# A decoder of two layers on one core: output chains in later slots, the first mixture's norm and router logits inside attention slots

## The reference, cut

```python
x = _layernorm(x + _L0_attn_ref(x, ...))          # window of 16 around a token, 16 heads of 8; token 0 sees all
x = _layernorm(x + _L0_xattn_ref(x, ctx, ...))    # causal self attention + attention on ctx, one output product
x = _layernorm(x + _L0_ffn_ref(x, ...))           # 16 experts, each takes its top 64 tokens of 1024
x = _layernorm(x + _L1_attn_ref(x, ...))          # gated linear recurrence and a gated MLP
x = _layernorm(x + _L1_xattn_ref(x, ctx, ctx, ...))
x = _layernorm(x + _L1_ffn_ref(x, ...))           # 8 experts, top 2 of them per token

# the opening of _L0_ffn_ref, which the change is about
rms = jnp.sqrt(jnp.mean(xf * xf, axis=-1, keepdims=True) + EPS)
xn = xf / rms * norm_weight
logits = xn @ router_weight.T + router_bias
_, idx = jax.lax.top_k(logits.T, top_k)           # top_k = 64
```

## Time and profile before

| | us |
|---|---|
| median of 3 timed runs | 622.6 |
| lowest, highest | 620.65, 623.71 |
| the profiled execution | 616.85 |
| its span, first to last instruction | 615.1 |

### The profile page before, as it was taken

The page is one execution under the profiler, slowest core; times in us unless marked ns, Lnnn a source line. Parts: engine busy times, 40 slices in busy tenths (PEclk is TensorE's granted clock), DMA queues, the critical chain, the costliest instruction groups (busy, mean ns, idle before and its releaser), DMA issues. The chain is left out here.

```text
span 615.1 us, 10513 instructions
## 1 busy us (share of the span) xinstructions
PE 503.2 (82%) x3848; PEld 239.5 (39%) x3848; DVE 382.2 (62%) x876; ACT 221.5 (36%) x447; POOL 182.3 (30%) x296
## 2 busy tenths in 40 slices
PE   3899988878989898852499957885998889789994
PEld 2445443333333333320159843363333333334441
DVE  7646756577675768147965678644478842255574
ACT  2213452454656556701012115222117654332221
POOL 7736365644473622125000025101434000000000
PEclk9999998999999999977789978896899986799998
DMA  6321012235411100025040022000311000425200
GB/s 229 89 61 52 4 52 55 69 114 165 140 54 52 36 19 3 3 67 243 2 138 2 2 66 89 0 2 14 90 52 53 4 3 0 143 64 150 58 17 18
DMA packets 26899, 38.03 MB, mean 62 GB/s; under 512 B 3648, under 2 KB 19520, under 8 KB 26464
## 3 DMA queue, kind: packets, MB, share of 16 engines
q1 hardware_dynamic: 26848, 37.36, 20.0%
HBM read 23.91 MB, written 0.59 MB: 40 GB/s over the span
## 5 line engine op out<-in xcount | busy, mean ns | idle before, releaser
L1052 DVE TENSOR_REDUCE nmax<-bank 128x2 f32<-128x512 f32 (+2 forms) x240 | 145.6, 625 | 80.6 <-PE bank L832 38.3
L940 ACT ACTIVATE arena<-bank 128x512 f32<-128x512 f32 (+2 forms) x256 | 130.0, 524 | 136.0 <-PE bank L836 94.6
L498 PE MATMUL bank<-causal_qk,identb 128*128 128x512 bf16 x309 | 99.6, 428 | 28.9 <-DVE moe_top L1330 16.0
L836 PE MATMUL bank<-arena 64*128 64x256 bf16 (+2 forms) x512 | 87.0, 262 | 1.6 <-ACT arena L940 1.5
L832 PE MATMUL bank<-arena 62*128 62x256 bf16 (+2 forms) x512 | 85.2, 258 | 3.6 <-DVE nmax L1052 3.2
L877 PE MATMUL bank<-arena 128*32 128x256 f32 (+4 forms) x1088 | 75.3, 356 | 7.2 <-ACT arena L940 4.4
L832 PEld LDWEIGHTS bank<-arena 62*128 62x128 bf16 x512 | 30.1, 95 | 67.5 <-issue 49.3
L498 PEld LDWEIGHTS bank<-causal_qk,identb 128*128 128x128 bf16 x309 | 28.4, 107 | 69.2 <-issue 42.8
L702 POOL TENSOR_SCALAR_AFFINE_SELECT arena<-arena 128x256 f32<-128x256 f32 x64 | 25.5, 407 | 55.8 <-ACT arena L940 55.1
L836 PEld LDWEIGHTS bank<-arena 64*128 64x128 bf16 x512 | 30.6, 95 | 19.6 <-issue 9.7
L877 PEld LDWEIGHTS bank<-arena 128*32 128x32 f32 x1088 | 21.6, 110 | 34.2 <-issue 20.1
(11 more groups left out here) (284 smaller groups left out, 819.5 us busy)
## 6 DMA issues: line engine op xcount, KB each, us to landing
arena<-arena SPq DMA_DIRECT2D x96, 128.0 KB, 2.4
fcw<-in_fc1T SPq DMA_DIRECT2D x16, 256.0 KB, 3.1
arena<-in_fc2T SPq DMA_DIRECT2D x1, 4096.0 KB, 15.1
arena<-comb_rows SPq DMA_DIRECT2D x16, 256.0 KB, 5.2
fcw<-in_last SPq DMA_DIRECT2D x1, 2304.0 KB, 8.5
arena<-pos_rows SPq DMA_DIRECT2D x16, 128.0 KB, 2.9
arena<-comb_rows SPq DMA_DIRECT2D x16, 128.0 KB, 4.6
w<-in_w SPq DMA_DIRECT2D x1, 1216.0 KB, 6.2
```

Of the source, the lines that this page charges most:

```text
L498: nc.tensor.matmul(bank[:, :], m.identb[:, :], m.causal_qk[:, 0:4, :], start=True, stop=True)
L836: sins = t.matmul(sout[i], stack_rows(m, nh, h, 1, SCORE_ROWS)[:, i * P:(i + 1) * P], stack_rows(m, nh, h, 0, SCORE_ROWS)[:, spans[i][0]:s ...
L940: s.activation(m.prob[h % 8][:, 0:w], score_bank(n, h)[:, 0:w], ACT.Exp).then_inc(exps, 1)
L1052: v.tensor_reduce(m.nmax[n % 2][:, qt, h0:h0 + nh], MX[c % NMX][:, 0:nh * (k1 - k0)].rearrange("p (h k) -> p h k", h=nh), AX.X, ALU.max, n ...
```

## The change

Three things.

1. The offsets ott, yt, out and x1t become a `Chain`, of which there are two: NEAR (59, 61, 63, 67, as before) and FAR (60, 63, 65, 70). Only job 0 of layer 0 keeps NEAR; all other jobs, those of layer 1 too, get FAR. The steps behind them (y, yT, z, power, x, xT) keep their distance to their slot. The slots of the Router in layer 1 move with x1t.
2. The opening of the first mixture leaves `expert_choice` and becomes a second helper, `Opening`, in the slots of layer 0, once for each sequence b: first = 16 (5 + 2b) + 69, that is one slot after the normed x of cross job 5 + 2b. first: squares, sum and mean (DVE); +1: power (POOL); +2: scaled x (DVE); +3: two transposes into M1 (PE); +4: copy with scale (ACT); +6: product with the router weights into M1 (PE); +7: copy with bias (ACT), into m.hid in place of xres. The transpose of the norm weights is at slot 140, its DMA at slot 120.
3. In `expert_choice` the product x times norm weight (for the experts' input, L1325 before) goes from DVE to POOL, ahead of POOL's splitting into three terms. The 12 keep_warm products there (F_NORM) go; 8 (F_LAST) stand ahead of the last two transposes in `Opening`.

```diff
-S_OUT, S_QK, S_QKE, S_SPLIT = 63, 0, 1, 3
-S_X1T = 67
-S_OTT, S_YT = 59, 61
+S_QK, S_QKE, S_SPLIT = 0, 1, 3
+Chain = namedtuple("Chain", "ott yt out x1t")
+OTT, YT, OUT, X1T = range(4)
+NEAR, FAR = Chain(59, 61, 63, 67), Chain(60, 63, 65, 70)
-F_LAST, F_NORM, F_GATED = 8, 12, 8
+F_LAST, F_GATED = 8, 8
+S_OPENED = 6
+S_NORM_COL = 140
+S_OPENING = [16 * (5 + 2 * b) + FAR.out + 4 for b in range(BATCH)]
-S_LOGITS = (S_X1T + 2, 16 + S_X1T + 2, 32 + S_X1T + 2)
-S_WEIGHTS = 16 + S_X1T + 5
-S_COMB = 99
+S_LOGITS = tuple(16 * n + FAR.x1t + 2 for n in range(3))
+S_WEIGHTS = 16 + FAR.x1t + 5
+S_COMB = 101
...
+class Opening:
...
+    def sync(self, sp, slot):
+        if slot == S_NORM_COL - 20:
+            sp.dma_start(self.wr[:, :], self.dram["routerT"]).then_inc(self.w_in, 16)
+            sp.dma_start(self.rb[:, :], self.dram["router_b"]).then_inc(self.w_in, 16)
+            sp.wait_ge(self.w_in, 32)
...
+            if slot == first + 1:
+                pool.wait_ge(self.ms_ready, b + 1)
+                self.nc.gpsimd.tensor_tensor(self.rms[:, ts], self.ms[:, ts], m.eps[:, 0:1].broadcast_to([P, QT]),
+                                             ALU.pow).then_inc(self.rs_ready, 1)
...
+        if slot == S_NORM_COL:
+            pe.wait_ge(self.m1_read, self.m1_no["norm_col", 0])
+            t.transpose(M1[:, 0:P], row(m, "moe_norm"), m.ident[:, :]).then_inc(self.m1_full, 1)
...
+            if slot == first + 3:
+                pe.wait_ge(self.m1_read, self.m1_no["xs", b])
+                if b == BATCH - 1:
+                    keep_warm(self.nc, m, M1, F_LAST)
+                pe.wait_ge(self.xs_ready, b + 1)
+                for q in range(QT):
+                    ins = t.transpose(M1[:, q * P:(q + 1) * P], m.x[1][:, QT * b + q, :], m.ident[:, :])
+                ins.then_inc(self.m1_full, 1)
+            if slot == first + 6:
+                pe.wait_ge(self.w_in, 32)
+                pe.wait_ge(self.m1_read, self.m1_no["logits", b])
+                t.matmul(M1[0:E0, 0:SEQ], self.wr[:, :], m.xT[0][:, b * SEQ:(b + 1) * SEQ], start=True, stop=True).then_inc(self.m1_full, 1)
...
+            if slot == first + 4:
+                act.wait_ge(self.m1_full, self.m1_no["xs", b] + 1)
+                s.activation(m.xT[0][:, sl], M1[:, 0:SEQ], ACT.Copy, scale=self.norm_col[:, :]).then_inc(self.m1_read, 1)
+            if slot == first + 7:
+                act.wait_ge(self.w_in, 32)
+                act.wait_ge(self.m1_full, self.m1_no["logits", b] + 1)
+                s.activation(self.logits[:, sl], M1[0:E0, 0:SEQ], ACT.Identity, bias=self.rb[:, :]).then_inc(self.m1_read, 1)
...
+            if slot == first:
+                dve.wait_ge(self.x1_ready, BATCH + b + 1)
+                link(v.tensor_tensor(self.sq[:, :, :], x2, x2, ALU.mult))
+                link(v.tensor_reduce(self.ms[:, ts], self.sq[:, :, :], AX.X, ALU.add))
+                v.tensor_scalar(self.ms[:, ts], self.ms[:, ts], 1.0 / D, MOE_EPS, ALU.mult, ALU.add).then_inc(self.ms_ready, 1)
+            if slot == first + 2:
+                dve.wait_ge(self.rs_ready, b + 1)
+                v.tensor_tensor(m.x[1][:, ts, :], x2, self.rms[:, ts].unsqueeze(2).broadcast_to([P, QT, D]),
+                                ALU.mult).then_inc(self.xs_ready, 1)
...
+    steps = [NEAR if tight and n == 0 else FAR for n in range(NJ)]
...
-                n = at(slot, S_OUT)
+                n = late(slot, OUT)
...
-    attention_pipeline(nc, m, jobs, "l0_", max_banks=3, side=lambda ctx: ClassToken(nc, m, dram, ctx), fill=F_FIRST)
+    attention_pipeline(nc, m, jobs, "l0_", max_banks=3, side=lambda ctx: [ClassToken(nc, m, dram, ctx), opening], fill=F_FIRST, tight=True)
...
-            pool.wait_ge(xnT_mm, 8)
-            pool.wait_ge(xn_ready, 1)
+            link(g.tensor_tensor(xn, m.x[1][:, :, :], row(m, "moe_norm").unsqueeze(1).broadcast_to([P, TILES, D]), ALU.mult))
             link(g.tensor_copy(xnl[:, 0], xn))
...
-            t.transpose(B[7][:, 0:P], row(m, "moe_norm"), m.ident[:, :]).then_inc(col_mm, 1)
-            keep_warm(nc, m, B[6], F_NORM)
-            pe.wait_ge(xs_ready, 1)
-            for i in range(TILES):
-                t.transpose(B[i // 4][:, (i % 4) * P:(i % 4 + 1) * P], m.x[1][:, i, :], m.ident[:, :]).then_inc(xnT_mm, 1)
-            pe.wait_ge(w_in, 80)
-            for c in range(2):
-                pe.wait_ge(xnT_in, c + 1)
-                t.matmul(B[2 + c][0:E0, :], wr[:, :], xnT[:, 512 * c:512 * c + 512], start=True, stop=True).then_inc(lg_mm, 1)
-            pe.wait_ge(lg_in, 2)
...
-            link(v.tensor_tensor(m.x[1][:, :, :], x2[:, :, :], x2[:, :, :], ALU.mult))
-            link(v.tensor_reduce(m.veps[:, :], m.x[1][:, :, :], AX.X, ALU.add))
...
-            dve.wait_ge(lg_in, 2)
             for i in range(CAP // 8):
                 src = logits if i == 0 else work
```

## The result

The changed kernel is **slower**: ratio to the kernel before 1.0151, 95% interval 1.0096 to 1.0205. Both intervals leave out "no change"; that the loss is as much as 2% is not shown. The ratio is larger than the medians because it is made from the runs within 1.5% of each kernel's fastest, and the kernel before had one at 606.94. I had forecast 617.0, in a range of 610.0 to 626.5, and a gain of 5.6.

What follows compares the result with a forecast made beforehand. TensorE was taken to set the pace, its output-chain waits costing time nearly one to one. The terms -5.7 + 2.3 + 4.8 - 4.2 - 2.8 = -5.6 took the median from 622.6 to 617.0 us, range 610.0 to 626.5.

Steps and rivals of the forecast that it cites:

- (a): End of layer 0, handover to the first mixture: chain only one sequence long, 5.7 us less (bounds 3.8 to 6.2).
- (b): Layer 0, moved output-chain steps: old waits go, new ones come, +2.3 us in sum (bounds -5.5 to +9).
- (c): Layer 0, the opening's steps for three sequences placed in the stream: +4.8 us (bounds 3.0 to 8.7).
- the ot waits: Layer 0, jobs 1 to 7: ot copy one slot later makes each of seven waits 0.7 us longer, +5.0.
- the yT step: Layer 0, wait for yT before the output product: 4.0 us go, 1.5 return through POOL's masks, net -2.5.
- (d): Layer 1: waits for yT, x and split maxima mostly go, -4.2 us (bounds -6.6 and 0).
- (e): TensorE's clock in layer 1: half clock after the removed waits costs 5.5 us, half of it taken, -2.8.
- slower: Rival, chance 0.20: new waits at M1 2.0 us each, not 1.15, no clock gain; +4.5 (627.1), +8.8 at worst.
- waits at M1: TensorE waiting for z before the maxima's transposes: 1.15 us forecast in most jobs, +5.8 in layer 0; over 1.8 favours "slower".

Runs made afterwards that it cites:

- near_l0: The changed kernel with layer 0's chains back at their old slots, the later slots kept in layer 1 only; mean 616.3 us, ratio to before 1.0030.
- open_late: near_l0 with every step of the mixture's opening one slot later; mean 617.4 us in 6 runs, no ratio.
- open_near: The changed kernel with every job's output chain, in both layers, at its old slots, only the opening moved; mean 619.0 us, ratio to before 1.0037.
- fill: The changed kernel with three keep_warm products put into each of twelve long TensorE waits of layer 0; mean 616.0 us, ratio to before 0.9972.
- both: open_late with keep_warm products laid under layer 0's waits; mean 612.6 us, ratio to before 0.9819.

## Why the prediction was wrong, point by point

(a) The handover: forecast -5.7, measured -4.65, within its bounds; most of the missing microsecond is TensorE's half clock, which I had put into the bounds as +0.9 and not into the sum. near_l0 and open_late have it at 5.0.

(b) and (c), layer 0 without its clock: forecast +2.3 and +4.8, +7.1 together. Measured by the rows, +4.1 of idle time and 3.0 of the opening's work on TensorE (its price, not a measurement): +7.1. The agreement is in part luck, since the sizes inside are off in both directions: the ot waits went from 4.9 to 10.9 in seven, +6.0 for my +5.0; z came to 6.6 for my 5.8; x -4.2 came as said, yT -4.0 for my net -2.5; y did not go, 2.0 in four up to 270 us after 1.8 in five; and a term was missing, GpSimd's masks at the product with v, 4.3 in place of 2.1. I had given 1.5 of this to the yT step. One place I had not seen at all: where the opening's power waits on GpSimd for VectorE's mean, the causal mask stands behind it, and the product with v waits 1.92:

```profile
267.58 0.69 POOL L480 TENSOR_TENSOR open_rms<-open_ms,eps 128x2 f32<-128x2 f32 x1 [1.28 <-DVE open_ms L529]
...
268.34 0.65 POOL L805 TENSOR_SCALAR_AFFINE_SELECT arena<-arena 128x256 f32<-128x256 f32 x1
...
269.14 0.64 PE L980 MATMUL bank<-arena 128*32 128x256 f32 x8 [1.92 <-POOL arena L805]
```

I had walked the moved steps past SP's queue and past VectorE's, and not past GpSimd's.

(d) and (e), layer 1: forecast -4.2 and -2.8, -7.0; measured -7.5 in the profiles, but the other way round. TensorE's idle time fell by 1.1 us only (12.6 to 11.5), since waits for z (1.3 in two) came for those that went, and those for the reductions and y grew (2.4 to 3.0 and 1.0 to 1.8); its busy time fell by 6.4, with the clock at 0.95 in place of 0.87. At equal half clock (10 us each) open_near has 98.9 and the changed kernel 96.8, so the later slots by themselves are worth some 2 us there. The other traces lean the same way: with the old slots in layer 1 there are three, of 104.3, 103.7 and 98.9 us with 27, 20 and 10 us of half clock; with the later slots there are eleven, of 95.5 to 97.7 us with 7 to 15. But over all runs the gain is no more than 2.6 +- 2.5 by near_l0 and open_near, and the clock of the whole program does not rise (0.918 and 0.920). The profiled execution of before was the one with the most half clock there, and I had made the sum against it.

**The step that failed is the clock, priced in (e) for layer 1 alone, and at nothing in (b) for layer 0.** I took -2.8 where the change takes waits away and, without a reason, no term where it puts waits in. Over all runs the clock of the whole program shows no gain, 0.913 before and 0.911 after, less than +1 us by the slope of 4.2 us for 0.01. In layer 0 the change replaced fifteen waits (for ot, x and yT), twelve of 0.6 to 0.9 and three of 1.0 to 1.9, by twelve of 1.1 to 1.9; in the profiled execution 32 us more of half clock and 15 us of time came with them.

By the means, the later slots of layer 0 cost 7.2 +- 4.1 us where (b) has 2.3; some 3 of the 7.2 are clock, by the slope. Layer 1 gave 2.6 +- 2.5 where (d) and (e) have 7.0, and the idle time of (d) was too high by itself (4.2 for 1.1 in the profiles). The opening with its handover gave 1.0 +- 2.5 where (a) and (c) have 0.9. From -5.6 to +3.6 these are +4.9, +4.4 and -0.1. So the clock is a part of the miss and not all of it; how large a part stays open within these intervals.

My rival "slower" had the right place, but a wrong price and point: it asked for waits at M1 of over 1.8 us, they were 1.1 to 1.5, and it did not name the clock. Its sum also counts the two waits of layer 1 twice (they are in the 8.3 and again in the 1.7), so it is +7.1 at the worst and +3.6 at half. That this is the measured difference is luck. The rule of the Trainium skill that I weighed (TensorE: Matmul & The Clock Gate, "Part 1: The HAM clock gate"), that the throttled state is the default and activity releases it, agrees with fill, where activity without use brought 0.92 to 1.00. I had applied it to one layer.

And the forecast was of a median, from one profiled execution which lay near the fast end of a spread of 24 us (606.9 to 631.0 in 114 runs). The difference of two profiled executions (+10.0) is no measure of the difference of the means (+3.6).

## What to carry to other kernels

Read the clock from many runs before it is given a price: the time at half clock in one profile is in part of that execution (27 us in layer 1 in one, 10 in another with the same slots there). When the clock is priced, price it on both sides, where waits go and where waits come; that several waits joined into one long one cost more than apart fits the profiles here, but no run holds the total and changes only the lengths. Before a step is moved later to take away a wait, look what fills the time now (here a keep_warm product and four transposes) and keep that ahead of the wait. Filling waits with products of no use gave 7.6 +- 3.7 us in the changed kernel and 7.1 +- 6.4 in the one before, while the rearrangement lost 3.6. When a wait is taken away and the stage gets no shorter, look which other engine is now waited for: here GpSimd's masks. And when an experiment gives time back, do it to the kernel before as well, or it does not tell what the change cost.

## What the runs showed of the hardware

Thirty-six more matmuls of 128x512 in layer 0 made the kernel 7.6 +- 3.7 us faster in the mean, with the granted clock from 0.911 to 0.935. Over 94 runs of one kernel, 0.01 of granted clock goes with 4.2 us of some 620. And a stretch in which TensorE counts as busy for 9.67 and 9.75 of 10 us, in the drain of both, stays at 0.55 and 0.50: there, being busy by that column was no sign that the clock would rise.
